# Cross attention over four batches: the turn of the next batch's context, of the first x tile and one copy of Y placed anew, with the query matmuls that fill the gaps

## The reference, cut to what matters

```
query = x @ Wq;  keyt = enc @ Wk;  valt = enc @ Wv
hs = mha(query, keyt, valt)                          # 2048 queries, 150 keys
ca_q1 = einsum('btc,th->bch', ca, Wq_ca)[:, indices, :]
ca_hs1 = mha(ca_q1, x, x)                            # 384 different queries, 2048 keys
ca_hs2 = mha(ca_hs1 @ Wq, ca @ Wk_ca, ca @ Wv_ca)    # 4 keys
out = (hs + ca_hs2) @ Wout + b_out + x
```

## Time and profile before

| what | value |
|---|---|
| median of 3 runs | 1592.3 us (1591.59 to 1593.23) |
| the profiled execution, its own time | 1591.0 us |
| its span in the profile | 1589.2 us |
| PE busy / PEld busy | 1530.4 us (96%) / 1254.2 us (79%) |
| DVE busy | 789.6 us (50%) |
| ACT busy | 623.4 us (39%) |
| mean granted clock of PE | 0.99 |
| one batch, from first key matmul to first key matmul | 386.0 us |

### The profile page before, as it was taken

The page is one execution under the profiler, slowest core; times in us unless marked ns, Lnnn a source line. Parts: engine busy times, 40 slices in busy tenths (PEclk is TensorE's granted clock), DMA queues, the critical chain, the costliest instruction groups (busy, mean ns, idle before and its releaser), DMA issues.

```text
span 1589.2 us, 24605 instructions
## 1 busy us (share of the span) xinstructions
PE 1530.4 (96%) x10294; PEld 1254.2 (79%) x10294; DVE 789.6 (50%) x1591; ACT 623.4 (39%) x1314; POOL 2.8 (0%) x12
## 2 busy tenths in 40 slices
PE   5999999999999999999999999999999999999999
PEld 4774589999976369999987538999998744899998
DVE  5677345343368543533447825334344782443533
ACT  1426723233143852322324484223233357332322
POOL 0000000000000000000000000000000000000000
PEclk9989999999999999999999999999999999999999
DMA  6530002130234001112025200114004510021101
GB/s 238 193 131 34 1 23 88 55 118 20 98 134 151 1 6 56 64 67 94 26 100 186 91 1 18 52 56 152 18 34 143 179 38 1 19 92 55 59 17 42
DMA packets 46680, 117.27 MB, mean 74 GB/s; under 512 B 3661, under 2 KB 5317, under 8 KB 45019
## 3 DMA queue, kind: packets, MB, share of 16 engines
q1 hardware_dynamic: 37036, 93.91, 16.8%
q10 hardware_dynamic: 9535, 21.80, 3.6%
HBM read 77.33 MB, written 39.17 MB: 73 GB/s over the span
## 4 chain that ended last, share of the span: by engine, by line
PE 82%; ACT 7%; DVE 7%; issue 2%; DMA 1%; SPq 0%; ACTq 0%
PE ps_w L492 41%; PE ps_s L492 17%; PE ps_t L492 15%; PE ps_t L502 9%; DVE unit_max L1247 4%; ACT work L1070 3%; ACT work L1040 1%; DVE ot L1413 1%; ACT ot L1102 1%; DMA xc<-in_L_xattn_Wout_dram 1%; ACT ot L986 0%; DMA y_all<-in_L_xattn_Wv_ca_dram 0%; PE ps_s L502 0%; PE ps_w L502 0%; ACT work L974 0%
## 5 line engine op out<-in xcount | busy, mean ns | idle before, releaser
L492 PE MATMUL ps_w<-wo_h,ot 128*128 128x320 f32 x1280 | 327.2, 321 | 1.0 <-DVE ot L1413 1.0
L1247 DVE TENSOR_REDUCE unit_max<-ps_s 128x1 f32<-128x512 f32 x384 | 239.8, 683 | 53.4 <-PE ps_s L492 52.6
L492 PEld LDWEIGHTS ps_w<-wo_h,ot 128*128 128x128 f32 x1280 | 222.5, 188 | 2.0 <-DVE ot L1413 2.0
L492 PE MATMUL ps_w<-wo_l,ot 128*128 128x320 f32 x640 | 197.7, 309 | 0.0
L1040 ACT ACTIVATE work<-ps_s,neg_max 128x150 f32<-128x150 f32 x512 | 161.0, 400 | 41.8 <-DVE neg_max L1305 41.8
L492 PE MATMUL ps_w<-v_all,work 120*128 120x162 f32 (+1 forms) x1280 | 171.3, 288 | 0.0
L492 PEld LDWEIGHTS ps_w<-v_all,work 120*128 120x128 f32 x1280 | 169.1, 191 | 0.8
L1031 ACT ACTIVATE work<-ps_t 120x512 f32<-120x512 f32 (+1 forms) x128 | 62.9, 491 | 226.1 <-PE ps_t L502 226.1
L502 PE MATMUL ps_t<-ident,work 128*120 128x128 f32 (+1 forms) x960 | 139.9, 276 | 2.0 <-DVE ot L1413 1.0
L492 PE MATMUL ps_s<-keys_h,qt_h 128*128 128x300 f32 (+1 forms) x448 | 134.8, 301 | 0.6
L1301 DVE TENSOR_REDUCE neg_max<-ps_s 128x6 f32<-128x900 f32 x64 | 70.1, 1095 | 126.9 <-PE ps_s L492 126.9
(11 more groups left out here) (159 smaller groups left out, 2230.1 us busy)
## 6 DMA issues: line engine op xcount, KB each, us to landing
xc<-in_x_dram SPq DMA_DIRECT2D x32, 1280.0 KB, 6.4
out_dram<-work ACTq DMA_DIRECT2D x64, 320.0 KB, 2.2
xt_all<-work SPq DMA_DIRECT2D x60, 256.0 KB, 2.2
xt_l<-xt_all SPq DMA_DIRECT2D x12, 1280.0 KB, 5.6
y_all<-in_L_xattn_Wk_dram SPq DMA_DIRECT2D x4, 960.0 KB
y_all<-in_L_xattn_Wv_dram SPq DMA_DIRECT2D x4, 960.0 KB
pick<-pick_all SPq DMA_DIRECT2D x16, 194.0 KB
xc<-in_L_xattn_Wq_dram SPq DMA_DIRECT2D x1, 1600.0 KB, 10.6
```

Of the source, the lines that this page charges most:

```text
L492: return nc.tensor.matmul(out, lhs, rhs, start=start, stop=stop, skip_group_check=True)
L1247: v.tensor_reduce(unit_max[:, a, n, q:q + 1], bank, AX_X, ALU.max).then_inc(max_free, 1)
```

## The change

It has four parts.

1. The turn of the context becomes a function `turn_ctx(b)`. For batch 0 it stands where it did. For the others it stands at the end of the batch before, ahead of the two projections of the last tile, and without a wait for `y_ready`; that wait now stands ahead of the turn of `cst`. It writes `ps_s` bank 2 in place of `ps_t` bank 0. ACT's two copies move as well (`take_ctx`), ahead of the stores of the last two output tiles.
2. x tile 0 is turned ahead of the last value piece, and ACT copies it ahead of taking that piece and ahead of its wait for the output stores. For that the ring begins at slot 7 (`xt_slot`), whose columns are not those of `enc_t` or `o_tile`.
3. The second bank of chunk 0's Y is copied by DVE, in `split_g(0)`, the first still by ACT. Chunks 1 to 3 stay as they were.
4. `Q0_FILL` holds other numbers, and step 6 joins `Q0_ENDS`: three query matmuls now stand between the turn of x tile 6 and the first product of chunk 1. The total is the same.

```diff
-Q0_FILL = [0] * 8 + [4, 4, 3, 2, 2, 3, 3, 3, 3, 3, 3, 3, 3]
-Q0_ENDS = (12, 17)
+Y_SHARED = (0,)
+Q0_FILL = [0] * 6 + [3, 0, 4, 3, 2, 1, 2, 4, 4, 2, 2, 3, 4, 4, 1]
+Q0_ENDS = (6, 12, 17)
...
+def xt_slot(m):
+    return (m + XT_FIRST) % XT_RING
...
-            for b in range(B):
+            def turn_ctx(b):
                 pe.wait_ge(kv_in, 16 * KV_LOADS * (b + 1))
-                pe.wait_ge(y_ready, START + b * NST)
                 for c in range(CT):
-                    turned(ps_t[:, 0, c * KEYS:c * KEYS + P], ctx_in[:, 0, c * P:(c + 1) * P])
-                    last = turned(ps_t[:, 0, c * KEYS + P:(c + 1) * KEYS], ctx_in[0:REM, 1, c * P:(c + 1) * P])
+                    turned(ps_s[:, 2, c * KEYS:c * KEYS + P], ctx_in[:, 0, c * P:(c + 1) * P])
+                    turned(ps_s[:, 2, c * KEYS + P:(c + 1) * KEYS], ctx_in[0:REM, 1, c * P:(c + 1) * P])
...
                 pe.wait_ge(cst_base, b + 1)
+                pe.wait_ge(y_ready, START + b * NST)
...
+                    if n == V_ORDER[-1]:
+                        pe.wait_ge(xc_in[0], 16 * (b * XC_LOADS + 1))
+                        turn_x(0, 0, piece_bank[("x", 0)], gx_turned)
...
+                if b + 1 < B:
+                    turn_ctx(b + 1)
                 project(SLOTS - 1, 0)
                 project(SLOTS - 1, 1)
...
+                for m in range(VT_HALF - 1):
+                    take_values(m)
+                copy_x(0)
+                take_values(VT_HALF - 1)
...
-                    for bank in range(2):
+                    for bank in range(1 if i in Y_SHARED else 2):
                         st = i * ST + 2 * bank
-                        nc.scalar.activation(y_all[:, st:st + 2, :, 0:GYW], gy(bank), copy).then_inc(y_copied, 1)
+                        nc.scalar.activation(y_all[:, st:st + 2, :, 0:GYW], gy(bank), copy).then_inc(y_copied[bank], 1)
...
+                if b + 1 < B:
+                    take_ctx(b + 1)
                 store(SLOTS - 2)
                 store(SLOTS - 1)
...
                 def split_g(i):
-                    dve.wait_ge(y_copied, (b * CHUNKS + i + 1) * 2)
+                    if i in Y_SHARED:
+                        dve.wait_ge(gx_used, b * GX + (i + 1) * KT)
+                        v.tensor_copy(y_all[:, i * ST + 2:(i + 1) * ST, :, 0:GYW], gy(1)).then_inc(y_copied[1], 1)
+                    for bank in range(2):
+                        dve.wait_ge(y_copied[bank], b * CHUNKS + i + 1)
```

More of the change, by code:

```diff
@@ L569, in _ @@
                 last.then_inc(enc_full, 1)
+            turn_ctx(0)
+            for b in range(B):
                 pe.wait_ge(enc_ready, 2 * (b + 1))
@@ L602, in products @@
                     if kt == 0 and i:
-                        pe.wait_ge(y_copied, (b * CHUNKS + i) * 2)
+                        for bank in range(2):
+                            pe.wait_ge(y_copied[bank], b * CHUNKS + i)
                     h0, hs, n0 = TILE_HEADS[kt][0], len(TILE_HEADS[kt]), PAIR_AT[(kt, TILE_HEADS[kt][0])]
@@ L946, in _, with take_ctx @@
             act.dma_start(pick_all, c_pick).then_inc(pick_out, 16)
-            for b in range(B):
+            def take_ctx(b):
                 act.wait_ge(enc_full, b + 1)
-                enc_psum = ps_t[:, 0, 0:CT * KEYS].rearrange("p (c k) -> p c k", c=CT)
+                enc_psum = ps_s[:, 2, 0:CT * KEYS].rearrange("p (c k) -> p c k", c=CT)
                 nc.scalar.activation(enc_t[:, :, 0:KEYS], enc_psum, copy).then_inc(enc_ready, 1)
                 nc.scalar.activation(enc_t[:, :, KEYS:ENC_W], enc_psum[:, :, 0:ENC_W - KEYS], copy).then_inc(enc_ready, 1)
+            take_ctx(0)
+            for b in range(B):
                 for a in range(PHASES):
@@ L954, in _, with take_values @@
                     nc.scalar.activation(ca_mat[:, a, :], ps_w[:, a, 0:CAD], copy).then_inc(ca_base_ready, 1)
-                for m, n in enumerate(V_ORDER):
+                def take_values(m):
+                    n = V_ORDER[m]
                     act.wait_ge(v_full, VT_HALF * b + max(m + 1, 2))
@@ L998, in _ @@
                     i, kt = divmod(m, KT)
-                    copy_x(m)
+                    if m:
+                        copy_x(m)
                     if 1 <= m <= KT:
                         act.wait_ge(xt_copied, b * GX + m)
-                        nc.scalar.activation(xt_h[:, m - 1, :], xt[:, m - 1, :], copy).then_inc(xt_high, 1)
+                        nc.scalar.activation(xt_h[:, m - 1, :], xt[:, xt_slot(m - 1), :], copy).then_inc(xt_high, 1)
                     if i and kt == 0:
@@ L1272, in _ @@
                     dve.wait_ge(xt_high, b * CHUNKS * KT + kt + 1)
-                    v.tensor_tensor(xt_l[:, kt, :], xt[:, kt, :], xt_h[:, kt, :], ALU.subtract).then_inc(xt_ready, 1)
+                    v.tensor_tensor(xt_l[:, kt, :], xt[:, xt_slot(kt), :], xt_h[:, kt, :], ALU.subtract).then_inc(xt_ready, 1)
                 split_g(0)
```

19 lines of the change are left out of this document (10 added, 9 removed).

## The result

| | before | after |
|---|---|---|
| median, same chip, four runs each | 1592.8 us (1591.6 to 1593.2) | **1574.8 us** (1572.0 to 1576.1) |
| the profiled execution, its own time | 1591.0 us | 1574.7 us |
| its span | 1589.2 us | 1572.9 us |

The ratio is 0.9887, with an interval from 0.9873 to 0.9901: 1.1% faster. The forecast was 1576.8 us, the range 1572.0 to 1583.0.

The account below looks back on a forecast made before the run. PE, busy 96% of the span, was taken as the bound, losing time to waits, hidden stalls and low clock. 6.6 + 5.1 + 0.2 + 1.2 + 2.4 = 15.5 us off 1591.0, plus 1.3 for the median: 1576.8 us, range 1572 to 1583.

Parts of the forecast that it names:

- The waits at the boundary: Three batch boundaries: turning the context early removes PE's waits, 2.2 us each, 6.6 us in all.
- the counted 1.84: Boundary waits as the profile counts them, 0.25 + 0.67 + 0.92 us; the lower end of the gain per boundary.
- The clock: Keys behind each boundary: without the gap at granted clock 1.00, 4.0 instead of 5.65 us; 5.1 us in all.
- The rule of the Trainium skill: Batch starts, rival A: clock falls only after much longer idle, so another cause; 5.1 us stay, 1581.9; chance 0.10.
- x tile 0 ahead: First product: waits for the last value piece instead of the x copy; 0.05 us a batch, 0.2 in all.
- The Y copy: Chunk 1's first product: starts later, but three query matmuls fill in; net 0.3 us a batch, 1.2 in all.
- The filler: Trios of units: new filler numbers cut stalls from 4.2 to 3.5-3.6 us a batch; 2.4 us in all.
- The walk through the new numbers: Trios: 0.12 too early at step 9, 0.36 stalls grow to 0.60, the largest shrinks from 0.78 to 0.24.
- The sum: Whole kernel: all terms together take 15.5 us off the profiled execution's 1591.0, to 1575.5.
- rival B: Batch 0's queries: the low clock stretch at 100 to 111 us goes too, 3.75 us; 1573.1; chance 0.30.
- D: Slower: more of twelve alike places (three per batch) get the low stretch, 3.7 us each; chances 0.07 and 0.02.

Follow-up runs that it names:

- the filled waits: Kernel before plus unread matmuls, three ahead of the y_ready wait and four behind the context's turn, in batches 1 to 3: 1588.8 us, ratio 0.9990.
- part 1 alone: Kernel before with only the context turned ahead of the last tile's projections: 1582.4 us, ratio 0.9941.

## Why the prediction was right

- **The waits at the boundary**, 2.2 each: measured 2.22 (8.05 - 4.80 - 1.03). The choice of start to start over the counted 1.84 was right. The context behind the projections splits it into 0.85 and 1.4, where the rows count 0.67 for the first and 0.92 + 0.24 for the second; a wait counted in a row leaves out the end of the row ahead of it.
- **The clock**, 1.7 each: measured 1.77, 1.77 and 1.66. The cause given was shown by filling the waits: keys at 3.88 us with the same distance and the same DMA share at the boundary. The rule of the Trainium skill that the prediction set against the row (page "TensorE: Matmul & The Clock Gate", table "Why this matters for your kernels": it names only much longer idle gaps as what brings the clock down) does not cover these falls, if idle means that PE stands still: two waits of 0.67 and 0.92 us with transposes between them were enough in six boundaries of six, and 0.92 behind the same transposes in one of three. What the same page of the Trainium skill says under "PE-mode transpose", that transposes don't count as busy in the way other matmuls do, fits both: PE did nothing but wait and transpose for 3.1 us ahead of the keys in before (1200.11 to 1203.19), and for 2.2 in the run with the context behind the projections (1190.20 to 1192.43). No run took the transposes away and left the waits.
- **x tile 0 ahead**, 0.05: 0.03, by the same exchange of waits.
- **The Y copy**: DVE's copy was taken as 0.62 us and took 0.62; the gap of 0.4 to 0.7 us was 0.58. The stage grew by 0.37 where 0.4 was said, and holds three fillers worth 0.7: net 0.33 against 0.3. What the prediction did not work out is the alternative that lay in its own rows. ACT alone, with its 0.97 us and the fillers beside it, lets the product go 0.4 us earlier than sharing does.
- **The filler**, 0.6: 4.15 - 3.50 = 0.65 by the trio rows, and 1.25 - 0.70 = 0.55 by the stage. The walk through the new numbers also named where stalls appear: 0.11 at step 9 (0.12 said), 0.36 that grow to 0.58 (0.60 said), the largest down to 0.32 (0.24 said).
- **The sum**, 15.5: 15.4 by the stages. The forecast lies 2.0 us above the median: 1.3 were added because the median of before stood that much above its profiled execution, which after's did not (0.1), and 0.9 us of low stretches went besides. That the whole time agrees so well is in part luck: in another set of runs the median of before was 1585.9 us, and two kernels of that set whose stages are within 0.4 us a batch of after's were at 1574.2 and 1574.7, 11 to 12 us less and not 18.

**What was wrong is the step on rival B**: that the low stretch of batch 0 "hangs on small shifts of time", so that an order either has it or loses it, with 3.7 us as its price. It did vanish, but the kernel before, run again, had it in another batch, and a shorter one at two places. The premise of D, "one of twelve alike places", comes out in part: all three times that the traces have this long stretch (before, its repeat, the filled waits) it began at the x tile behind the tenth trio, which is behind the last of the three turns of `gst` that D counts in a batch, so at one place a batch and not three. What neither B nor D had is that each execution draws anew which batches get one. B should have been no case with a time of its own but a spread of some microseconds around every case, and its gain of 3.7 was partly made up by 1.1 + 1.1 + 1.8 elsewhere.

## What to carry to other kernels

A short wait ahead of a block of matmuls can cost twice, itself and the lower clock level behind it; look at the windows' granted clock right behind each gap, and when only the clock is in question, fill the wait with unread matmuls to see which of the two it is. Before a copy is shared between two engines, look at what stands in the second engine's queue at that moment: here the start of its half decided, not the length. And when whole times wander by more than the edit is worth, judge edits by stages from start to start in batches whose clock stayed up, and compare where the low stretches begin across several traces before calling them random.

## What was not expected of the hardware

The clock stands at its lower level in stretches in which PE is busy without a gap: for 23.7 us at 23.70 busy in the run with the old filler, for 10.1 in the repeated before. In which batches they come changes from one execution to the next of the same kernel, but where in the batch they begin hardly does. The thirteen traces of this case hold 39 such stretches between the keys and the last projections. Of these 3 begin at the x tile behind the tenth trio (before, its repeat and the filled waits, each about 10 us long), 15 within 2.4 us behind the start of the twelfth trio, 19 in the scores of the second branch, 5 to 11 us behind their start, and 2 ahead of the first trio (both in the run with the old filler). In the eight traces with the new filler none is longer than 6.8 us, while four of the five with the old one have one of 10 us or more; whether the order does this was not tested.

Two of them were read closely. Ahead of the one in the repeated before stood transposes and a trio of units on 12 rows, with a wait of 0.34 us; ahead of the one in the repeated after, matmuls on 28 and 32 rows with a wait of 0.19. For the latter windows of PE in batch 1 read

```profile
503.50:507.50 4.00, 3.71 (x25) 1.00 0.67 282
507.60:511.00 3.40, 3.40 (x23) 0.50 0.00 0
```

so PE was busy 3.71 of 4.00 us ahead of the fall, much of it in such small rows. A low stretch cost 1.1 us there and 1.6 to 9 us among the queries. What decides in which execution it comes is open: no run here separated the small rows from the short waits. Taking the boundary's falls away did not take these away: in two kernels (part 1 alone, the filled waits) the profiled execution had two and four of them in the middle of batches, where the two executions of before had one and three. Whether that is an exchange or chance is open too.
